# Cross-attention and a low-rank mixture of experts on one core: the mixture prepares its next block a stage later with two gains rows, roots stand next to their measurement, and ScalarE moves the first halves

## The reference

```python
# x, ctx: (4, 1024, 1024); 8 heads of 128 rows in each of 4 batches
x = x + gamma * xattn(layernorm(x), ctx, ctx)
x = x + ffn(layernorm(x), U, V, W1, b1, W2, b2)

# xattn, heads over rows: qh, kh, vh are (b, 8, 128, 1024)
qk  = einsum('bhdq,bhdl->bhql', qh, kh) / sqrt(128)
ret = einsum('bhql,bhdl->bhdq', softmax(qk), vh)

# ffn: 8 experts of rank 64
h     = relu(x @ W1 + b1)
alpha = softmax(h @ W2 + b2)
out   = einsum('bsk,bskd->bsd', alpha, U_k (V_k x))
```

## Time and profile before

| | |
|---|---|
| median of 3 runs | 1567.72 us (1561.28 to 1570.95) |
| the profiled execution | 1568.06 us, of which the span is 1566.3 us |
| busy, of the span | TensorE 1499.1 us (96%), VectorE 1055.6 (67%), ScalarE 824.4 (53%), GpSimd 744.1 (48%) |
| mean granted TensorE clock | 0.989 |
| DMA queue of SyncE | 288.21 MB, 59.7% of 16 engines' span |
| DMA queue of ScalarE | 47.72 MB, 8.8% |

### The profile page before, as it was taken

How to read it: one execution, slowest core, us unless ns; L and a number is a source line. 1 busy time by engine, 2 the same in 40 slices (tenths; PEclk the granted TensorE clock), 3 DMA queues, 4 the chain that set the end, 5 groups by cost and what they waited for, 6 DMA issues and landing times.

```text
span 1566.3 us, 20147 instructions
## 1 busy us (share of the span) xinstructions
PE 1499.1 (96%) x6216; PEld 1150.4 (73%) x6216; DVE 1055.6 (67%) x1287; ACT 824.4 (53%) x1266; POOL 744.1 (48%) x470
## 2 busy tenths in 40 slices
PE   5999999999999999999887799999999999999999
PEld 3776667777777777777565677878777787777877
DVE  7999999999999999999653444354454435445212
ACT  5888888888889898898741111121221122211120
POOL 2888888888888898888632200202011020200200
PEclk9999999999999999999998899999999999999999
DMA  5889989999889988998972464654637455364403
GB/s 162 261 284 312 298 293 314 280 276 281 265 278 276 287 271 276 280 273 254 303 262 60 140 218 135 199 176 128 199 111 246 129 167 189 118 218 134 134 0 108
DMA packets 144395, 336.46 MB, mean 215 GB/s; under 512 B 29408, under 2 KB 49120, under 8 KB 144352
## 3 DMA queue, kind: packets, MB, share of 16 engines
q1 hardware_dynamic: 126784, 288.21, 59.7%
q10 hardware_dynamic: 17568, 47.72, 8.8%
HBM read 136.36 MB, written 50.59 MB: 119 GB/s over the span
## 4 chain that ended last, share of the span: by engine, by line
PE 58%; DMA 14%; DVE 13%; SPq 9%; issue 3%; ACT 1%; POOL 1%; ACTq 0%; DVEq 0%; POOLq 0%
PE scores L571 14%; PE scores L1095 12%; PE attended L600 10%; DMA gain_wide<-gains 5%; PE spare L1139 5%; SPq L259 5%; PE scores L1139 5%; PE attended L1157 5%; PE attended L603 4%; DVE pb L645 4%; DVE neg_max L636 3%; DMA pt<-pb 2%; DMA result<-x 2%; DVE first_n L1208 2%; DMA out<-result 2%
## 5 line engine op out<-in xcount | busy, mean ns | idle before, releaser
L354 POOL TENSOR_TENSOR pt_lo<-pt,pt_hi 128x512 fp32r<-128x512 f32 x254 | 471.6, 1871 | 100.1 <-ACT pt_hi L424 99.2
L445 ACT ACTIVATE probs<-scores,neg_max 128x1024 f32<-128x1024 f32 x256 | 285.5, 1115 | 102.0 <-DVE neg_max L636 101.9
L645 DVE STREAM_TRANSPOSE pb<-probs 128x1024 f32<-128x1024 f32 x256 | 315.2, 1231 | 20.2 <-DMA pt<-pb 17.2
L636 DVE TENSOR_REDUCE neg_max<-scores 128x1 f32<-128x1024 f32 x256 | 308.9, 1207 | 21.9 <-PE scores L571 21.3
L571 PE MATMUL scores<-k_hi,q_hi 128*128 128x512 f32 x512 | 210.8, 493 | 26.5 <-ACT probs L445 16.1
L1039 ACT ACTIVATE hidden<-scores,b_col 128x512 f32<-128x512 f32 x64 | 44.1, 689 | 344.0 <-PE scores L1095 344.0
L424 ACT ACTIVATE pt_hi<-pt 128x512 fp32r<-128x512 f32 (+1 forms) x256 | 214.6, 838 | 0.0
L990 POOL TENSOR_TENSOR rstd<-var_eps,minus_half 128x1 f32<-128x1 f32 x28 | 18.2, 659 | 391.2 <-DVE var_eps L1227 391.2
L1095 PE MATMUL scores<-nt_hi,w_hi 128*128 128x512 f32 x512 | 202.2, 395 | 0.0
L1095 PE MATMUL scores<-nt_hi,w_lo 128*128 128x512 f32 x512 | 201.3, 393 | 0.0
L1095 PE MATMUL scores<-nt_lo,w_hi 128*128 128x512 f32 x512 | 201.1, 393 | 0.0
(11 more groups left out here) (108 smaller groups left out, 2600.8 us busy)
## 6 DMA issues: line engine op xcount, KB each, us to landing
pt<-pb SPq DMA_DIRECT2D x512, 256.0 KB, 5.4
attended_rows<-att_out SPq DMA_DIRECT2D x64, 256.0 KB, 5.5
result<-x SPq DMA_DIRECT2D x64, 256.0 KB, 4.2
out<-result SPq DMA_DIRECT2D x64, 256.0 KB, 3.0
k_raw<-in_ctx ACTq DMA_DIRECT2D x30, 512.0 KB, 5.8
x_raw<-in_x ACTq DMA_DIRECT2D x30, 512.0 KB, 6.6
first_n<-attended_rows SPq DMA_DIRECT2D x28, 512.0 KB, 4.2
gain_wide<-gains SPq DMA_DIRECT2D x28, 512.0 KB, 4.3
```

What stands on the lines that cost most here:

```text
L354: nc.gpsimd.tensor_tensor(pt_lo[2 * parity + half][:, :, keys, :], pt[2 * parity + half][:, :, keys, :], as_f32(hi[half][q][:]), ALU.subtr ...
L445: nc.scalar.activation(probs[j % 2][:], scores[j % 2][:], ACT.Exp, bias=neg_max[:, j:j + 1], accum_out=row_sum[b][:, j:j + 1]).then_inc(s_ ...
L636: nc.vector.tensor_reduce(neg_max[:, j:j + 1], scores[j % 2][:], AX_X, ALU.max, negate=True).then_inc(s_max, 1)
L645: nc.vector.transpose(pb[half][:, :, j % HALF, :], probs[j % 2][:]).then_inc(s_blocks, 1)
```

## The change

1. In attention's heads 3 to 10 the loads and the store of own halves (`load_own`, `store_own`) go from SyncE's program to ScalarE's: the store at j = 2, the loads at j = 3. Before, they stood between SyncE's `send_gain` and its gather of half 0.
2. In head 31 the load of tiles 2 and 3 moves behind the store of head 29's half 0 (`store_attended(h - 2, 0)`) and `send_gain`. first_statistics(0) moves from j = 5 to j = 7, first_statistics(1) behind the last turn. GpSimd's roots follow one place later (`first_factor(0)` ahead of the first `low_probs` behind the loop). Tiles 0 and 2 are normalised by VectorE (a subtraction and a multiplication), tiles 1 and 3 by ScalarE. TensorE's transposes come one block later.
3. In the mixture there are two gains rows and two x rows per pair (`gain_wide` becomes two buffers; the second gains row and the second x row lie in the memory of `result`). `scale_and_add`, `measure`, `normalise` of tiles 0 and 1 come one stage later, tile 3 is scaled after the softmax. `turn_squares(0)` stands right behind `normalise(0)`.
4. On SyncE: `u_raw` is loaded behind the first gains and x rows of group 0; from group 1 on a wait for the four `s_out` stands ahead of the second gains row; the alpha store and the first two alpha rows come ahead of the store of tile 3 (in group 0 of tiles 2 and 3) and of the residual loads.
5. In group 0 GpSimd computes the root of tile 0 ahead of the splits of U, that of tile 1 after two of them; W1's chunks 6 and 7 are split at stage 2.

```diff
@@ sync, attention
-            if own_at(h - 1 if known else h) is not None:
-                store_own(own_at(h - 1))
-            if own_at(h) is not None:
-                load_own(own_at(h))
             gather(h, n, 0, parity)
-            if last:
-                load_first(n, (2, 3))
             if not (known and h < 2):
                 store_attended(h - 2, 0)
             send_gain(h, 0)
+            if last:
+                load_first(n, (2, 3))
@@ gpsimd, attention
-                if last and j == 6:
-                    first_factor(0)
...
         for j in range(JB):
             if j == 0:
-                first_factor(1)
+                first_factor(0)
             if j < JB - 1:
                 low_probs(quarter_in(h, n, j, 0, LOW_LAG))
-            if j in (1, 2):
+            if j < 3:
                 first_factor(j + 1)
@@ scalar, attention
+                if j == 2 and own_at(h - 1 if known else h) is not None:
+                    store_own(own_at(h - 1))
+                if j == 3 and own_at(h) is not None:
+                    load_own(own_at(h))
...
-                if last and j == 7:
-                    normalise_first(0)
...
-            if j >= 1:
-                first_high(j - 1)
-            if j in (0, 2, 4):
-                normalise_first(j // 2 + 1)
+            if j >= 2:
+                first_high(j - 2)
+            if j in (1, 3):
+                normalise_first(j)
+        first_high(JB - 2)
@@ tensor, attention
-            if j >= 1:
-                turn_first(j - 1)
+            if j >= 2:
+                turn_first(j - 2)
...
-            if j == 0:
-                turn_first(JB - 1)
+            if j < 2:
+                turn_first(JB - 2 + j)
@@ vector, attention
-                if last and j in (5, 7):
-                    first_statistics(j // 2 - 2)
+                if last and j == 7:
+                    first_statistics(0)
...
         inverse_sums(h - 1, 1, 1)
+        normalise_first(0)
+        first_statistics(1)
         first_statistics(2)
         first_statistics(3)
+        normalise_first(2)
@@ mixture
-    gain_wide = lent.tensor("gain_wide", [P, D])
-    x_wide = [lent.tensor(f"x_wide{b}", [P, D]) for b in range(2)]
+    gain_wide = [lent.tensor("gain_wide0", [P, D])]
+    x_wide = [lent.tensor("x_wide0", [P, D])]
...
+    gain_wide.append(top_lent.tensor("gain_wide1", [P, D]))
+    x_wide.append(top_lent.tensor("x_wide1", [P, D]))
...
-    W1_AT = ((1, 2), (3, 4, 5), (6,), (7,), (), (), (), ())
-    VU_AT = ((), (), (8,), (9,), (10, 11), (12, 13), (14, 15), ())
+    W1_AT = ((1, 2), (3, 4, 5), (6, 7), (), (), (), (), ())
+    VU_AT = ((), (8,), (9,), (10, 11), (), (12, 13), (14, 15), ())
@@ sync, mixture
                 if first:
-                    sp.dma_start(u_raw[:], shared["u_dram"]).then_inc(s_u_in, 16)
                     for s in shared["s_att"]:
                         sp.wait_ge(s, 16 * tiles)
                 else:
+
                     sp.wait_ge(s_y[1], g * GT)
-                load_gain(t, g, 0)
                 for k in range(2):
+                    if not first and k == 1:
+                        for b in range(4):
+                            sp.wait_ge(s_out[b], g * 32)
+                    load_gain(t + k, g, k)
                     load_x(t + k, g, k)
-                load_gain(t + 1, g, 1)
+                if first:
+                    sp.dma_start(u_raw[:], shared["u_dram"]).then_inc(s_u_in, 16)
...
-                load_gain(t + 3, g, 3)
-                store_x1(t + 2, g, 2)
+                if not first:
+                    store_x1(t + 2, g, 2)
+            store_alpha(g)
+            for r in range(2):
+                spread_alpha(g, r)
+            if not last:
+                if first:
+                    store_x1(t + 2, g, 2)
                 store_x1(t + 3, g, 3)
             for i in range(4):
                 load_residual(g, i)
-            store_alpha(g)
-            for r in range(RB):
+            for r in range(2, RB):
                 spread_alpha(g, r)
@@ gpsimd, mixture, group 0
-                for n in range(KB, KB + 6):
+                for n in range(KB, KB + 4):
                     low_weights(n)
                 factor(g, 0)
+                low_weights(KB + 4)
+                low_weights(KB + 5)
+                factor(g, 1)
                 low_weights(KB + 6)
-                factor(g, 1)
@@ vector, mixture: hidden_stage (groups 1 to 6)
-            if e == 1:
-                scale_and_add(g, 0)
...
             if e == 2:
-                scale_and_add(g, 1)
...
+                scale_and_add(g, 0)
+            if e == 3:
...
+                turn_squares(g, 0, False)
+            if e == 5:
+                normalise(g, 1)
+                turn_squares(g, 1, False)
+            if e == 7:
+                scale_and_add(g, 2)
@@ vector, mixture: first_hidden_stage (group 0)
+            if e == 3:
+                scale_and_add(g, 0)
+            if e == 4:
+                scale_and_add(g, 1)
+                measure(g, 0)
+            if e == 5:
+                measure(g, 1)
+                normalise(g, 0)
                 turn_squares(g, 0, True)
+            if e == 6:
                 normalise(g, 1)
@@ vector, mixture: slot
             if not last:
                 if first:
                     scale_and_add(g, 2)
-                    scale_and_add(g, 3)
+                scale_and_add(g, 3)
                 measure(g, 2)
```

More of the change, by code:

```diff
@@ L817, in mixture @@
     s_vuhi, s_vulo = sem("s_vuhi"), sem("s_vulo")
-    s_gain_wide, s_mult, s_sum = sem("s_gain_wide"), sem("s_mult"), sem("s_sum")
+    s_gain_wide = [sem(f"s_gain_wide{b}") for b in range(2)]
+    s_mult, s_sum = sem("s_mult"), sem("s_sum")
     s_xin, s_x1 = ([sem(f"{name}{b}") for b in range(2)] for name in ("s_xin", "s_x1"))
@@ L886, in load_gain @@
         def load_gain(t, g, k):
-            if not (isinstance(g, int) and g == 0 and k == 0):
-                sp.wait_ge(s_mult, g * GT + k)
-            sp.dma_start(gain_wide[:], scratch[bass.ts(t, 2), :].rearrange("a n -> (a n)")
-                         .partition_broadcast(P)).then_inc(s_gain_wide, 16)
+            if k >= 2:
+                sp.wait_ge(s_mult, g * GT + (k - 1))
+            sp.dma_start(gain_wide[k % 2][:], scratch[bass.ts(t, 2), :].rearrange("a n -> (a n)")
+                         .partition_broadcast(P)).then_inc(s_gain_wide[k % 2], 16)
         def load_x(t, g, k):
@@ L905, in load_residual @@
             b = i % 4
-            if not (isinstance(g, int) and g == 0 and i < 4):
+            if i >= 4:
                 sp.wait_ge(s_out[b], g * 32 + (i // 4) * 16)
+            elif isinstance(g, int) and g == groups - 1:
+                sp.wait_ge(s_out[b], g * 32)
             sp.dma_start(result[b][:], x1[bass.ts(g * GT + i // 2, P), i % 2 * BANK:(i % 2 + 1) * BANK]
@@ L959, in slot @@
                 load_x(t + 3, g, 3)
+                load_gain(t + 3, g, 3)
                 gather(g, 0)
@@ L1337, in slot @@
                 if not last:
-                    if e == (3 if first else 2):
+                    if e == (4 if first else 3):
                         variance(g, 0)
-                    if e == (4 if first else 3):
+                    if e == (5 if first else 4):
                         variance(g, 1)
```

72 lines of the change are left out of this document (34 added, 38 removed).

## The result

The changed kernel takes 1577.99 us (median of 4, 1576.75 to 1580.11), the kernel before 1567.6 (median of 4): a ratio of 1.0072, 95% interval 1.0039 to 1.0106. So it is slightly slower and, at the 1% that the forecast set, no change. The profiled execution has a span of 1575.0 us against 1566.3. 1540 was forecast, so some 38 us are to be found.

What follows compares the result with a forecast made beforehand. TensorE, busy nearly all the time, was taken as the bound, losing time in waits and low clock. Span: 1566.3 - 27.5 + 3.4 - 2.0 - 1.5 = 1538.7, so a median of 1540 us, range 1523 to 1557.

Steps and rivals of the forecast that it cites:

- What bounds the kernel: Whole kernel: TensorE is busy nearly all the time; only its waits and slow-clock stretches can be won, mainly in group 0.
- Group 0's three waits: Mixture, group 0 stages: TensorE's waits from a late gains row and two late roots would go, 14.3 us.
- Group 0, -27.5: Mixture, first group: stage waits and their clock loss go, a 3.6 us wait stays; length 97.8 us, or -27.5.
- Own halves, -1.5, bounds 0 and -6: Attention heads 3 to 10: moving own-half issues to ScalarE starts the half-0 gather up to 2.2 us earlier; -1.5 us.
- Groups 1 to 6, +3.4: Mixture: 7.1 us of waits go, but a new 1.75 us wait in each of six groups adds 10.5.
- 0.43 us per us of wait: Mixture, group 0: slow-clock work per us of TensorE wait, from 9.9 us of clock loss and 22.8 of waits.
- Rival C: Groups 1 to 6: longer new wait, store landing 4.6 us, clock lowered; +20.2 for +3.4, 1557 us; chance 0.18.
- End of attention, -2.0, bounds 0 and -3.5: From attention's end to the first hidden product: moved loads, stores and normalisations bring that product from 782.0 to 780.0.
- term for strides: End of attention: a normalisation moved to VectorE was taken at 2.0 us for its strides, against 0.8 at unit stride.
- E: Mixture: tile 3's store lands as late as the first gains row, 9.8 us; slower, 1610 us; chance 0.06.
- D: Group 0 not cured: two of three waits stay, 10 us and 4 of clock; 1554 us; chance 0.08.
- B: Mixture: no new wait before the expert products, as `gt_lo` has unseen slack; 1524 us; chance 0.15.

Runs made afterwards that it cites:

- e1_own_back: The changed kernel with the own halves' loads and stores back on SyncE at their old place, behind the second-half gather: 1556.91 us, ratio 0.9944.
- e2_own_alone: The kernel before with only the own halves' loads and stores moved to ScalarE: 1590.02 us, ratio 1.015.
- e4_own_sp_first: The changed kernel with the own halves on SyncE at the head's start, ahead of the second-half gather: 1565.49 us, ratio 0.9987.
- e5_small_aside: e1_own_back plus four small transfers a head (16 KB in all) on ScalarE at the changed kernel's places for the own halves: 1560.62 us, ratio 0.9954.
- e6_last_tile_late: e1_own_back with VectorE's normalisation of each group's fourth tile behind the four gates, except in the last group: 1561.96 us, ratio 0.9967.
- e10_spreads_first: e1_own_back with SyncE issuing the third and fourth pair of factor rows ahead of the four residual loads: 1553.15 us, ratio 0.9911.
- e7_mixture_alone: The kernel before's attention, own halves on SyncE, with the changed kernel's mixture: 1556.89 us, ratio 0.9923.
- e9_both_late: e6_last_tile_late with SyncE also issuing the third and fourth pair of factor rows ahead of the residual loads: 1530.70 us, ratio 0.9763.
- e3_own_act_late: The changed kernel with the own halves' four issues still on ScalarE but one step later, at j == 4: 1578.07 us, ratio 1.008.

## Why the prediction was wrong

*What bounds the kernel*: right. Group 0's three waits went by the mechanisms named; two short ones for `ht_lo`, 0.8 us in all, are left.

*Group 0, -27.5*: measured -26.2 (99.1 us for 97.8). The wait for `gt_lo` is 0.5 + 2.8 for 3.6; the clock was granted at 0.98.

*Own halves, -1.5, bounds 0 and -6*: here is the failed step, 22 us. "Mostly for half 1, whose issue was never behind the moved ones" is true and was the wrong question. I asked what the moved DMAs had stood in front of, and took what gains from their leaving. The half-1 gather stood in front of *them*, and the move took them out from behind it. The row for it was there: the gathers' wait of up to 1.5 us, eight times, says that VectorE already stood for this transfer, so bytes new among its pieces had no slack to go into. From the gather's first issue to VectorE's block 0.7 MB more was moved, in 15.8 us (187.7 to 203.5, 252 GB/s) where it was 13.3 before (153.4 to 166.7, 246 GB/s). The median piece of that gather landed 6.7 us after its issue, for 5.3 before. 1 MB at 300 GB/s is 3.5 us; 2.6 us a head were lost. That the bytes and their place make most of it is shown by `e1_own_back`, `e2_own_alone`, `e4_own_sp_first` and `e5_small_aside`; ScalarE's issues have a part of at most some 4 us. The Trainium skill ("DMA: Bandwidth & Descriptors", section "Issuing engines are not separate DMA queues") has it that DMAs of all issuers run on the same 16 DMA engines and interleave there. The trace agrees: the DMA share is 1.03 while VectorE waits, in the stretch 

```profile
200.00:204.00 4.00, 3.46 (x15) 2.52 (x14) 0.36 (x1) 3.56 (x5) 2.04 (x1) 1.00 1.03 375
```

I drew from it only that nothing is gained by another issuer. That they interleave also means that another issuer's transfers are not kept behind those of SyncE.

*Groups 1 to 6, +3.4*: the mechanism was right (`ht_lo` gone, a wait for `gt_lo` once a group, VectorE idle for a store), and a term was mis-sized: +13.4. The store of tile 3 was to land in 3.2 us, between 2.9 and 4.6; issued at 964.73 in group 1, it landed 5.4 us later and kept normalise(3) until 970.19. The rows for the bounds came from another place in the queue, without four residual loads right behind. gate(0) is 69.2 us behind the group's start, not 68.1. So the wait is 2.2 to 2.7 us (in group 1 with one of 0.9 ahead of it) for 1.75, in six groups 14.6 in place of 10.5. Against the 7.1 removed that is 7.5 of the 13.4; the rest is TensorE's busy time, 560.8 us for 555.5. Part of it came with the clock. It was granted below 1.00 behind the waits of 2.8, 2.7 and 2.3 us of groups 0 to 2, here of the first two:

```profile
881.00:885.00 4.00, 4.00 (x15) 3.06 (x13) 0.61 (x2) 1.33 (x2) 3.54 (x2) 0.76 0.00 0
979.00:983.00 4.00, 4.00 (x13) 3.17 (x12) 0.59 (x2) 1.56 (x2) 3.31 (x2) 0.64 0.00 0
```

Behind the waits of 2.2 us in groups 3 to 6 it stayed at 1.00. The length of the wait does not settle it: in `e1_own_back` the clock stayed at 1.00 behind waits of 2.58 and 2.90 us (1147.69, 1243.35) and was 0.66 behind one of 2.14 (1436.21). So the sum's 0.43 us per us of wait is a mean of group 0 and no price of a single wait. And for gate(0) I had named one cause, the normalisation, where `e6_last_tile_late` and `e10_spreads_first` show two in series. Rival C, a longer wait with the clock down, came true in kind, at about 10 us of its 17: groups 1 to 6 took 13.4 more where it had 20.2.

*End of attention, -2.0, bounds 0 and -3.5*: about 0 in `e1_own_back` beside `e7_mixture_alone`, the upper bound, and 0.9 lost in the changed kernel's own trace. The pauses of 3 us came as said, twice (5.8 us), and the clock was at half from about 777 to 787. New are two waits for VectorE, 0.8 us for `pt_lo` and 0.9 for `w_lo`; they stand in `e1_own_back`, `e9_both_late` and `e10_spreads_first` too, and in `e7_mixture_alone`, with VectorE's old order there, neither does. "VectorE idles there" had no price for them. The normalisation that moved to VectorE took 3.01 us for tile 0, where the bounds were 0.8 and 2.0, and 1.55 for tile 2:

```profile
773.72 3.01 DVE L695 TENSOR_SCALAR first_in_order<-first_n,first_mean_var,first_rstd 128x1024 f32<-128x1024 f32 x1
782.98 1.55 DVE L695 TENSOR_SCALAR first_n<-first_n,first_mean_var,first_rstd 128x1024 f32<-128x1024 f32 x1
773.44 2.34 POOL L329 TENSOR_TENSOR pt_lo<-pt,pt_hi 128x1024 fp32r<-128x1024 f32 x1
782.26 1.29 POOL L329 TENSOR_TENSOR pt_lo<-pt,pt_hi 128x512 fp32r<-128x512 f32 x1
779.00:784.00 5.00, 2.41 (x6) 1.93 (x7) 4.27 (x11) 4.09 (x4) 4.90 (x6) 0.50 1.02 394
```

It is one line of code with the same strides both times, so the strides do not make the 3 us. Each time it starts while GpSimd works on a `pt_lo`, and ends 0.95 and 0.98 us after that one ends (775.78 and 783.55). The eleven experiments with this code have the same distance, 0.94 to 0.98 us, for both tiles, at lengths from 1.47 to 3.01 us; the one exception, tile 2 in `e3_own_act_late`, started 0.1 us ahead of its `pt_lo` and took 1.26 us. The sum's term for strides was thus the wrong term: about 1 us for the operation, and a stand beside GpSimd that the prediction priced at nothing.

*Rivals*: E did not come, D neither, B's missing wait came in groups 1 to 6 only once both orders were mended (1.6 us stay in group 0). None had a term for the heads, though the last sentence of the prediction named them as what would refute it. A part costed at -1.5 with a bound of -6 on one side and 0 on the other had no bound for a loss, and no reason to exclude one was given beyond the order of issue.

Open: why the third gate's rows came 1.2 us later in `e6_last_tile_late` than in `e1_own_back`, and what part of the store's 5.4 us is due to the residual loads behind it. The 4 us of `e5_small_aside` are not settled either, nor is the part of two queues side by side in the changed kernel's loss.

## What to carry to other kernels

When a DMA is moved to another engine, ask what it stood *behind*, not only what stood behind it: in heads whose DMA engines were busy 0.93 of the time, the order of issue was a priority, and the transfer that VectorE stood for paid for bytes put among or ahead of its pieces (1 MB: 2.6 us a head on another engine, 4.7 in the midst of the gather on the same one, 0.8 ahead of it). When a wait has been cured and the time stays, look at who else releases the waiting instruction: the gates had two releasers in series, and either cure alone moved the time by 4 or 5 us, up or down, while both were worth 26 us. And give each moved part a bound on the side of loss.

## What the hardware showed that was not expected

Issuing a DMA is not of one price, and on a compute engine it is compute time. The issue of `k_raw` on ScalarE rose from a median of 0.33 us before to 1.41 in the changed kernel, without being moved itself. In `e3_own_act_late` the load of the own half took ScalarE 2.83 us at 198.40, with a median of 0.72 in seven; SyncE's took 0.47 in the median before. Full DMA engines alone do not explain the long ones: at 164 to 165 us of the kernel before the DMA share was 1.10, and SyncE issued in 0.62 and 0.39 us. In `e3_own_act_late` SyncE was issuing a gather at the same time (197.31 to 206.08). Which of the two it takes is not shown.

A `TENSOR_SCALAR` of 128x1024 on VectorE that started while GpSimd worked on a large `TENSOR_TENSOR` ended only some 0.5 us (unit stride) or 0.95 us (permuted read and write) after that one. In the mixture of the changed kernel 26 of 28 took 0.81 us (L1261); the two that started beside a split of U, at 837.13 and 843.31, took 2.31 and 2.80, and the one that did so before, at 836.47, 2.75. Those that started beside a root (128x1) took 0.81. No run took GpSimd's operation away to see the length fall, so the cause is read from this coincidence, which has no exception in the traces of both kernels.
